# Graph layer on one core: the query rows of 56 of 98 edge tiles come by indexed gather instead of a spreading product, and two bulk blocks are handled earlier

## The chip, the core and the metric

The kernel runs on one core of a Trainium2 chip. The metric is the device time of one execution in microseconds (us), as the median of several runs. Lower is better. TensorE (PE) multiplies matrices, ScalarE (ACT) and VectorE (DVE) work on tiles of 128 partitions, GpSimd (POOL) here mostly issues indexed DMAs, and SyncE (SP) issues plain DMAs.

## What is computed

Two graph layers over 50,000 nodes with 256 features and 12,500 edges sorted by destination. Only nodes that have an incoming edge get more than a constant added:

```python
h = jnp.maximum(_layernorm(x, axis=-1), 0.0)
x = x + _L0_gnn_ref(h, L0_gnn_weight, src, dst, edge_weight)   # relu(segment_sum(w * (h @ W)[src], dst))
h = jnp.maximum(_layernorm(x, axis=-1), 0.0)
x = x + _L1_gnn_ref(h, ...)
# in _L1_gnn_ref:
Q = (h @ Wq).reshape(n, H, HD); K = (h @ Wk)...; V = (h @ Wv)...        # H = 8 heads of 32
score = jnp.einsum('ehd,ehd->eh', Q[dst], K[src]) / np.sqrt(HD)
score = score + jax.nn.relu(efeat @ W1 + b1) @ W2 + b2
alpha = softmax of score over the edges of one dst
out = jax.ops.segment_sum(alpha[:, :, None] * V[src], dst, num_segments=n)
return out.reshape(n, D) @ Wo + bo
```

## The kernel before

The edges are padded to `T = 98` tiles of 128 edges (`P`), in `G = 14` groups of `J = 7` tiles. A run is the set of neighbouring edges with one destination; what belongs to a destination (its x1, its h2, its q row) is complete only in the row of the run's last edge, its *end row*. The program has four stages, each written out in a fixed order for each engine; semaphores tie the engines together.

1. **Edges** (0 to about 363 us in the profile). For each tile: gather of x rows, normalisation, the first layer, second normalisation, q rows. x1, h2 and q are written to DRAM (`x1_d`, `h2_d`, `q_d`). After this stage GpSimd waits until all of h2 is stored.
2. **Pairs** (about 368 to 618 us), the loop `for t in range(T + 1)` on PE and ACT, `pairs` on DVE. For each tile t GpSimd gathers 128 rows of `h2_d` by source into `store` (`fetch`, index `slot_i`). PE transposes them (two products on `ident`), ACT copies the result to `hT`, PE makes K (bank 6 or 7) and V (bank 2 or 3) with `Wkv`, ACT copies V over `store`, DVE multiplies K by the q row of each edge's destination (`prod`, counted by `k3`) and sums over each head.

   Where the q rows come from: SP loads the group's rows of `q_d` linearly into `ringA` (`q_in`). There only end rows are right, so PE *spreads* them: a product of a 0/1 matrix `same` (DVE, `same_run`, from the positions of the end rows, `run_ends`) with the tile in `ringA` puts into each edge's row the end row of its run (bank 0 or 1), and ACT copies it to `msg`. A run that goes on in the next tile has its end row elsewhere; for that case GpSimd gathers one row per tile (`q_open`, index `end_i`), SP writes these rows over row 127 of each tile in `q_d`, and for the first 14 tiles a second time into `ringA` (`open_to`), for which PE waits before its first spread.
3. **Softmax** over runs (about 618 to 669 us), while the last bulk blocks are moved.
4. **Attend** (about 670 us to the end): weighted V, running sums, product with `Wo`, and GpSimd scatters the rows of each tile to `out`.

**Bulk.** Independent of the edges, out = x + bo is made for all nodes in 44 blocks ("units") of 9 rows per partition (1152 KB each): `bulk_load`, `add_bo`, `bulk_store`, in buffers of a rotation (`bulk_at`). Units 0 to 13 have their add on GpSimd in the edges stage, units 14 (`EARLY`) to 37 on DVE in the pairs stage (`add_unit` at j = 2 and j = 5 of a group, as many as `units(g)` has), 38 (`MIDDLE`) to 43 are filled with bo by ACT (`fill`) and added to by an accumulating load of GpSimd's queue. On SP, a bulk store waits for its add, and the load two units later is written behind it.

The rings: `ringA` holds 14 tiles (`A(u)`); gathers into `store` stay at most 14 tiles ahead of PE's transposes (`need(pool, t3, t - 2 * J + 1)`).

Of the kernel before, what the change touches and what calls it, by code (L numbers as in the profile page):

```python
# [8 lines left out]
P = 128  # L9
# [27 lines left out]
def gnn_program(nc, x, dst, src, wgt, eattr, W, Wq, Wk, Wv, W1, b1, W2, b2, Wo, bo, out):  # L37
# [9 lines left out]
    h2_d = nc.dram_tensor("h2", (EP, D), f32, kind="Internal").ap()  # L47
    q_d = nc.dram_tensor("q", (EP, D), f32, kind="Internal").ap()
    srcf_d = nc.dram_tensor("src_f", (T, P), u16, kind="Internal").ap()
    end_d = nc.dram_tensor("run_end", (EP,), bf16, kind="Internal").ap()  # L50
# [3 lines left out]
    with ctx:  # L54
        def sb(name, shape, dt=f32):
            return ctx.enter_context(nc.sbuf_tensor(name, shape, dt))
# [4 lines left out]
        def sem(name):  # L61
            return ctx.enter_context(nc.semaphore(name))
# [34 lines left out]
        slot_i = sb("slot_gather", [P, T], i32)  # L97
        end_i = sb("run_end_after", [T, 1], i32)
        row_no = sb("row_no", [P, 1])
        sc_all = sb("scores", [P, J, G, H])  # L100
# [66 lines left out]
        def group(ring, b):  # L167
            return ring[:, b * J * D:(b + 1) * J * D].rearrange("p (j d) -> p j d", d=D)
# [4 lines left out]
        def keys_ps(j):  # L173
# [28 lines left out]
        ql, end_in = sem2("q_loaded"), sem2("run_ends_in")  # L202
        s_end, end_out, open_in, open_out, open_to = (sem(n) for n in (
            "run_ends_ready", "run_ends_in_dram", "open_q_in", "open_q_in_dram", "open_q_in_ring"))
        same_rdy, qs, qc = (sem(n) for n in ("same_run_ready", "q_spread_in_psum", "q_spread_ready"))
        lag3, s_bo, s_reach = sem("dve_lag3"), sem("bo_parts_step"), sem("reach_of_carries")
        rb_free = sem("masks_in_ringB_used")
        s_flag, x_ps, x_sb, s_sm, pe_sm, act_sm, al_ps, s_al = (sem(n) for n in (
# [64 lines left out]
        def units(g):  # L273

            k = MIDDLE - EARLY
            return range(EARLY + k * g // G, EARLY + k * (g + 1) // G)

# [38 lines left out]
        def _(sp):  # L316
# [80 lines left out]
            def q_in(a):  # L397
                sp.dma_start(group(ringA, a % 2), edge_rows(q_d, a)).then_inc(ql[a % 2], 16)

            sp.wait_ge(keys, T)  # L400
            for a in range(2):
                ends_in(a)
            bulk_load(EARLY)
            bulk_load(EARLY + 1)
            sp.wait_ge(h1, T)
            for i in range(2):
                sp.wait_ge(st_q[i], 32)
            for a in range(2):
                q_in(a)
            for a in range(2):  # L410
                sp.wait_ge(ql[a], 16)
            sp.wait_ge(open_in, 16)
            sp.dma_start(q_d.rearrange("(t p) d -> t p d", p=P)[:, P - 1, :], q_open).then_inc(open_out, 16)
            sp.wait_ge(open_out, 16)
            sp.dma_start(ringA[P - 1:P, :].rearrange("o (u d) -> o u d", d=D),
                         q_d.rearrange("(t p) d -> p t d", p=P)[P - 1:P, 0:2 * J, :]).then_inc(open_to, 16)
            bulk_load(EARLY + 2)
            sp.wait_ge(x1r, T)
# [8 lines left out]
            for g in range(G):  # L427
                for u in units(g):
                    bulk_store(u)
                    if EARLY < u < MIDDLE - 2:  # L430
                        bulk_load(u + 2)
                if g + 2 < G:
                    sp.wait_ge(same_rdy, g + 1)
                    ends_in(g + 2)
                    sp.wait_ge(qs, J * (g + 1))
                    q_in(g + 2)
# [15 lines left out]
        def _(pool):  # L452
# [47 lines left out]
            for i in range(2):  # L500
                for part in range(2):
                    pool.wait_ge(st_h[part][i], 16 * (G // 2))
            for t in range(T):
                if t == 4:
                    for i in range(2):
                        pool.wait_ge(st_q[i], 16 * G)
                    fetch(q_open, q_d, end_i[:, 0:1], open_in)
                need(pool, t3, t - 2 * J + 1)
                u = t % (2 * J)
                fetch(store[:, t * D:(t + 1) * D], h2_d, slot_i[:, t:t + 1], o_in[u],  # L510
                      bounds_check=EP - 1, oob_is_err=False)

# [16 lines left out]
        def _(act):  # L529
# [111 lines left out]
            for t in range(T + 1):  # L641
                if t < T:
                    act.wait_ge(t3, t + 1)
                    need(act, kv, t - 1)
                    nc.scalar.copy(hT[t % 2], bank[4 + t % 2][:, 0:D].rearrange("p (c e) -> p c e", c=NC)).then_inc(hT3, 1)
                if t > 0:
                    act.wait_ge(qs, t)
                    need(act, k3, t - 2)
                    nc.scalar.copy(msg(t - 1), bank[(t - 1) % 2][:, 0:D]).then_inc(qc, 1)
                    act.wait_ge(kv, t)  # L650
                    nc.scalar.copy(store[:, (t - 1) * D:t * D], bank[2 + (t - 1) % 2][:, 0:D]).then_inc(v3, 1)  # L651
# [33 lines left out]
        def _(dve):  # L685
# [62 lines left out]
            def edges(g, h, b, on):  # L748
# [21 lines left out]
                def slots(j):  # L770
# [14 lines left out]
                    ins.then_inc(keys_rd, 1)  # L785

                for j in range(J):
                    u, t = b * J + j, J * g + j
# [58 lines left out]
            def same_run(a):  # L847

                dve.wait_ge(end_in[a % 2], 16 * (a // 2 + 1))
                need(dve, qs, J * (a - 1))  # L850
                nc.vector.tensor_scalar(same[a % 2], run_ends[a % 2], row_no[:, :], None, ALU.is_equal).then_inc(same_rdy, 1)
# [15 lines left out]
            def pairs(g, h, b, on):  # L867
# [16 lines left out]
                if g == 0:  # L884
                    same_run(0)
                for j in range(J + 1):
                    if j < J:
                        t = J * g + j
                        dve.wait_ge(kv, t + 1)
                        dve.wait_ge(qc, t + 1)  # L890
                        nc.vector.tensor_tensor(prod[:, j, :], bank[6 + t % 2][:, 0:D], msg(t), ALU.mult).then_inc(k3, 1)  # L891
                    if j == 3 and g + 1 < G:
                        same_run(g + 1)
# [122 lines left out]
        def _(pe):  # L1016
# [10 lines left out]
            pe.wait_ge(s_nxt, 2)  # L1027
            mm(bank[7][0:T, 0:1], line[:, 2, 1:T + 1], one_row[0:1, 0:1]).then_inc(s_tr, 1)
            pe.wait_ge(pdve, 12)
            pe.wait_ge(s_mlp, 144)  # L1030
# [91 lines left out]
            for t in range(T + 1):  # L1122
# [112 lines left out]
```

## Time and profile before

| | |
|---|---|
| median of 3 runs | 818.31 us (816.94 to 819.22) |
| the profiled execution | 815.25 us, span 813.1 us |
| busy share PE, DVE, ACT, POOL | 85%, 71%, 58%, 62% |
| mean granted TensorE clock | 0.963 |

The span is the time from the first to the last instruction in the trace; 815.25 - 813.1 = 2.15 us lie around it. Busy shares are averages over four stages with different limits.

### The profile page before, as it was taken

To read this page: it belongs to the slowest core of one execution; us is meant where nothing else is said; L and a number is where in the kernel's file an instruction comes from. 1 tells how busy PE (TensorE), PEld (TensorE's weight loads), DVE (VectorE), ACT (ScalarE), POOL (GpSimd) and SP (SyncE) were. 2 spreads that over 40 slices of the span, in tenths; PEclk is the share of its full clock that TensorE was granted. 3 is DMA by queue.
4 is the path that set the end of the run, shared out by engine and by line. 5 is a ranking of instruction groups with operands and counts; after the bars stand their busy time and mean duration, and the time that the engine had idled before them with its cause. 6 is when DMAs were issued, how large, how long until landed. Compare 5 with 4: busy or idle time off the path is not lost.

```text
span 813.1 us, 13370 instructions
## 1 busy us (share of the span) xinstructions
PE 694.8 (85%) x3804; PEld 546.8 (67%) x3804; DVE 580.4 (71%) x1676; ACT 467.7 (58%) x1383; POOL 506.1 (62%) x429
## 2 busy tenths in 40 slices
PE   1578999999799899962999999999998759999990
PEld 0346666666566667742878888888887637777770
DVE  5598888888877676700587565566567859999990
ACT  1557888887588789750444444444446276777700
POOL 6788887788878865206767576566402005777773
PEclk9989999999999999995999999999999978999996
DMA  6688999999989999696479799799796995766751
GB/s 176 212 272 261 335 326 338 354 356 334 321 246 340 312 341 357 231 358 202 151 258 329 275 362 355 283 328 374 253 351 187 269 316 168 222 202 215 231 170 52
DMA packets 122581, 224.01 MB, mean 276 GB/s; under 512 B 27475, under 2 KB 100828, under 8 KB 112142
## 3 DMA queue, kind: packets, MB, share of 16 engines
q1 hardware_dynamic: 74238, 150.45, 54.1%
q0 software_dynamic: 20464, 45.19, 18.6%
q10 hardware_dynamic: 27808, 27.53, 9.7%
q8 instruction: 32, 0.52, 0.2%
q14 instruction: 39, 0.32, 0.1%
HBM read 133.06 MB, written 102.76 MB: 290 GB/s over the span
## 4 chain that ended last, share of the span: by engine, by line
PE 49%; DVE 19%; DMA 15%; ACT 6%; issue 5%; POOL 3%; ACTq 1%; SPq 0%; DVEq 0%; POOLq 0%
PE bank L1018 43%; DVE small L1002 9%; DMA q<-ringC 5%; PE bank L1128 3%; DMA ringB<-x 2%; ACT ringB L623 2%; DVE small L801 2%; DVE store L991 2%; DMA work<-in_x 2%; PE bank L1109 2%; POOL out_x L522 2%; DMA ringA<-in_x,first_src 2%; DVE ringA L982 2%; PE bank L1084 1%; DMA out_x<-work 1%
## 5 line engine op out<-in xcount | busy, mean ns | idle before, releaser
L472 POOL DMA_INDIRECT store<-h,slot_gather x98 | 141.0, 1439 | 107.5 <-PE bank L1128 53.4
L1018 PE MATMUL bank<-Wkv_sb,small 128*128 128x256 f32 x784 | 186.6, 381 | 1.7 <-issue 1.7
L1018 PEld LDWEIGHTS bank<-Wkv_sb,small 128*128 128x128 f32 x784 | 149.9, 191 | 22.8 <-issue 2.1
L522 POOL DMA_INDIRECT out_x<-store,out_scatter x98 | 97.2, 991 | 52.5 <-issue 42.7
L472 POOL DMA_INDIRECT ringC<-in_x,dst_gather x98 | 92.7, 946 | 40.9 <-issue 25.6
L891 DVE TENSOR_TENSOR work<-bank,msgs 128x256 f32<-128x256 f32 x98 | 41.3, 422 | 107.6 <-PE bank L1018 107.6
L651 ACT COPY store<-bank 128x256 f32<-128x256 f32 x98 | 36.5, 372 | 134.3 <-PE bank L1018 134.3
L1018 PE MATMUL bank<-Wo_sb,small 128*128 128x256 f32 x392 | 109.7, 404 | 4.4 <-DVE small L1002 4.4
L679 ACT ACTIVATE ringA<-store,scores 128x32 f32<-128x32 f32 x392 | 87.6, 307 | 33.4 <-PE bank L1196 29.5
L1018 PE MATMUL bank<-W_sb,small 128*128 128x256 f32 x392 | 104.0, 389 | 0.0
L1018 PE MATMUL bank<-Wq_sb,small 128*128 128x256 f32 x392 | 101.5, 382 | 1.7 <-ACT ringC L555 1.6
L472 POOL DMA_INDIRECT ringA<-in_x,src_gather x84 | 79.6, 948 | 24.9 <-issue 19.7
L1002 DVE TENSOR_TENSOR_SCAN small<-flags,small,bank 128x128 f32<-128x128 bf16 x196 | 83.0, 466 | 4.2 <-PE bank L1196 3.6
L801 DVE TENSOR_TENSOR_SCAN small<-flags,small,bank 128x128 f32<-128x128 bf16 x196 | 82.8, 464 | 0.6 <-issue 0.3
L1018 PEld LDWEIGHTS bank<-Wo_sb,small 128*128 128x128 f32 x392 | 69.1, 197 | 16.3 <-DVE small L1002 7.4
L1018 PEld LDWEIGHTS bank<-Wq_sb,small 128*128 128x128 f32 x392 | 67.4, 192 | 7.6 <-issue 2.4
L1018 PEld LDWEIGHTS bank<-W_sb,small 128*128 128x128 f32 x392 | 68.8, 196 | 5.5
L776 DVE SCALAR_TENSOR_TENSOR bank<-bank,src_col,iota 128x128 f32<-128x128 f32 x98 | 34.3, 350 | 53.5 <-PE bank L1018 48.4
L305 POOL TENSOR_TENSOR bulk<-bulk,bo_all 128x2304 f32<-128x2304 f32 x14 | 71.2, 5085 | 0.3
L610 ACT ACTIVATE store<-ringA,nm,rs 128x256 f32<-128x256 f32 x98 | 57.2, 602 | 19.8 <-DVE nm L810 19.8
L1109 PE MATMUL bank<-ident,msgs 128*128 128x128 f32 x196 | 39.7, 285 | 20.7 <-DVE small L801 11.2
L623 ACT ACTIVATE ringB<-ringB,nm,rs 128x256 f32<-128x256 f32 x98 | 54.0, 593 | 1.2 <-DVE nm L836 0.6
(184 smaller groups left out, 1271.0 us busy)
## 6 DMA issues: line engine op xcount, KB each, us to landing
out_x<-bulk SPq DMA_DIRECT2D x33, 1152.0 KB, 7.6
bulk<-in_x SPq DMA_DIRECT2D x30, 1152.0 KB, 9.7
ringA<-q SPq DMA_DIRECT2D x14, 896.0 KB, 10.3
ringB<-x SPq DMA_DIRECT2D x12, 896.0 KB, 5.6
out_x<-ringC SPq DMA_DIRECT2D x9, 1152.0 KB, 6.5
ringC<-in_x SPq DMA_DIRECT2D x8, 1152.0 KB
x<-ringB SPq DMA_DIRECT2D x14, 512.0 KB, 5.9
h<-ringB ACTq DMA_DIRECT2D x14, 512.0 KB, 5.3
```

Of the source, the lines that this page charges most:

```text
L305: ins = eng_ops.tensor_tensor(v, v, bob[0:piece.shape[0], None, :].to_broadcast([piece.shape[0], rows_n, D]), ALU.add)
L472: pool.indirect_dma_start(to, None, table, bass.IndirectOffsetOnAxis(ap=at, axis=0), **more).then_inc(landed, 16)
L522: pool.indirect_dma_start(out, bass.IndirectOffsetOnAxis(ap=out_i[:, t:t + 1], axis=0), store[:, t * D:(t + 1) * D], None, bounds_check=N ...
L610: nc.scalar.activation(store3[:, J * a + k:J * a + k + 1, :], A(ab * J + k)[:, None, :], ACT.Relu, bias=nm1[:, ab, k:k + 1], scale=rs1[:, ...
L623: nc.scalar.activation(B(u), B(u), ACT.Relu, bias=nm2[:, lb, k:k + 1], scale=rs2[:, lb, k:k + 1]).then_inc(h2r, 1)
L651: nc.scalar.copy(store[:, (t - 1) * D:t * D], bank[2 + (t - 1) % 2][:, 0:D]).then_inc(v3, 1)
L679: ins = nc.scalar.activation(A(t % (2 * J))[:, n * HD:(n + 1) * HD], store[:, at:at + HD], ACT.Copy, scale=sc_all[:, t % J, t // J, n:n + 1])
L801: ins = nc.vector.tensor_tensor_scan(aT[u % 2][:, c, :], goes_on(u), bank[0][:, c * P:(c + 1) * P], aT[(u + 1) % 2][:, c, P - 1:P], ALU.mu ...
L891: nc.vector.tensor_tensor(prod[:, j, :], bank[6 + t % 2][:, 0:D], msg(t), ALU.mult).then_inc(k3, 1)
L1002: ins = nc.vector.tensor_tensor_scan(aT[u % 2][:, c, :], goes_on(u), bank[u % 2][:, c * P:(c + 1) * P], aT[(u + 1) % 2][:, c, P - 1:P], AL ...
L1018: return nc.tensor.matmul(o, lhsT, rhs, start=start, stop=stop)
L1109: ins = nc.tensor.transpose(bank[0][:, c * P:(c + 1) * P], msg(u + 1)[:, c * P:(c + 1) * P], ident[:, :])
```

## The change

- A tile t is now *spread* only if t >= 14 and t is even (42 tiles, `spread`). For the 56 others (`q_at` picks the column of the index table `qg_i`) GpSimd gathers the q rows of the end rows straight into `ringA`, 4 tiles behind its gathers into `store` (`lead`), and DVE multiplies K by `ringA` directly. PE's spreading product and ACT's copy to `msg` are gone for these tiles.
- `qg_i` is made at the start: PE transposes `w_last` into bank 4, DVE copies 14 and 42 columns of it.
- `q_in` loads only the rows of the spread tiles of groups 2 to 13, 127 rows of each, and the 128th from a table of its own, `open_d`. `same_run` runs for groups 2 to 13. The chain by way of `q_d` and `open_to` is gone.
- Units 14 and 15 are added to by DVE before its first tile, stored by SP before it waits for the last stores of q, and units 16 and 17 loaded behind that. `units(g)` shares out 22 units, not 24.

```diff
         def units(g):
-            k = MIDDLE - EARLY
-            return range(EARLY + k * g // G, EARLY + k * (g + 1) // G)
+            k = MIDDLE - EARLY - 2
+            return range(EARLY + 2 + k * g // G, EARLY + 2 + k * (g + 1) // G)
+        def spread(t):
+            return t >= 2 * J and t % 2 == 0
+        def spreads(t):
+            return max(0, (t - 2 * J + 1) // 2)
+        def q_at(t):
+            return t if t < 2 * J else J + t // 2
+        def q_landed(t):
+            return 16 * (T // (2 * J) + t // (2 * J) + 1)
...
             def q_in(a):
-                sp.dma_start(group(ringA, a % 2), edge_rows(q_d, a)).then_inc(ql[a % 2], 16)
+                rows_in = group(ringA, a % 2)[:, a % 2::2, :]
+                sp.dma_start(rows_in[0:P - 1], edge_rows(q_d, a)[0:P - 1, a % 2::2, :]).then_inc(ql[a % 2], 16)
+                sp.dma_start(rows_in[P - 1:P], open_d[J * a + a % 2:J * (a + 1):2, :][None, :, :]).then_inc(ql[a % 2], 16)
             sp.wait_ge(keys, T)
-            for a in range(2):
+            for a in (2, 3):
                 ends_in(a)
-            bulk_load(EARLY)
-            bulk_load(EARLY + 1)
-            sp.wait_ge(h1, T)
+            for u in range(EARLY, EARLY + 2):
+                bulk_load(u)
+            for u in range(EARLY, EARLY + 2):
+                bulk_store(u)
             for i in range(2):
-                sp.wait_ge(st_q[i], 32)
-            for a in range(2):
-                q_in(a)
-            for a in range(2):
-                sp.wait_ge(ql[a], 16)
+                sp.wait_ge(st_q[i], 16 * G)
+            for u in range(EARLY + 2, EARLY + 4):
+                bulk_load(u)
             sp.wait_ge(open_in, 16)
-            sp.dma_start(q_d.rearrange("(t p) d -> t p d", p=P)[:, P - 1, :], q_open).then_inc(open_out, 16)
-            sp.wait_ge(open_out, 16)
-            sp.dma_start(ringA[P - 1:P, :].rearrange("o (u d) -> o u d", d=D),
-                         q_d.rearrange("(t p) d -> p t d", p=P)[P - 1:P, 0:2 * J, :]).then_inc(open_to, 16)
-            bulk_load(EARLY + 2)
+            sp.dma_start(open_d, q_open).then_inc(open_out, 16)
...
-                    sp.wait_ge(same_rdy, g + 1)
-                    ends_in(g + 2)
-                    sp.wait_ge(qs, J * (g + 1))
+                    if g == 0:
+                        sp.wait_ge(open_out, 16)
+                    if g >= 2:
+                        sp.wait_ge(same_rdy, g - 1)
+                        ends_in(g + 2)
+                        sp.wait_ge(qs, spreads(J * (g + 1)))
+                    else:
+                        sp.wait_ge(k3, J * (g + 1))
                     q_in(g + 2)
...
-            for t in range(T):
-                if t == 4:
+            lead = 4
+            for t in range(T + lead):
+                if t < T:
+                    need(pool, t3, t - 2 * J + 1)
+                    fetch(store[:, t * D:(t + 1) * D], h2_d, slot_i[:, t:t + 1], o_in[t % (2 * J)],
+                          bounds_check=EP - 1, oob_is_err=False)
+                v = t - lead
+                if v == 0:
                     for i in range(2):
                         pool.wait_ge(st_q[i], 16 * G)
+                    pool.wait_ge(h1, T)
+                    pool.wait_ge(s_qg, 1)
+                if v >= 0 and not spread(v):
+                    need(pool, k3, v - 2 * J + 1)
+                    fetch(A(v % (2 * J)), q_d, qg_i[:, q_at(v):q_at(v) + 1], x_in[v % (2 * J)])
+                if v == 5:
                     fetch(q_open, q_d, end_i[:, 0:1], open_in)
...
                 if g == 0:
-                    same_run(0)
+                    for u in range(EARLY, EARLY + 2):
+                        add_unit(u)
...
-                        dve.wait_ge(qc, t + 1)
-                        nc.vector.tensor_tensor(prod[:, j, :], bank[6 + t % 2][:, 0:D], msg(t), ALU.mult).then_inc(k3, 1)
+                        if spread(t):
+                            q_rows = msg(spreads(t))
+                            dve.wait_ge(qc, spreads(t) + 1)
+                        else:
+                            q_rows = A(t % (2 * J))
+                            dve.wait_ge(x_in[t % (2 * J)], q_landed(t))
+                        nc.vector.tensor_tensor(prod[:, j, :], bank[6 + t % 2][:, 0:D], q_rows, ALU.mult).then_inc(k3, 1)
...
-                    if v % J == 0:
-                        pe.wait_ge(same_rdy, v // J + 1)
-                        pe.wait_ge(ql[v // J % 2], 16 * (v // J // 2 + 1))
-                        pe.wait_ge(open_to, 16)
-                    need(pe, qc, v - 1)
-                    mm(bank[v % 2][:, 0:D], same[v // J % 2][:, v % J * P:(v % J + 1) * P], A(v % (2 * J))).then_inc(qs, 1)
+                    if spread(v):
+                        a, n = v // J, spreads(v)
+                        if v < J * a + 2:
+                            pe.wait_ge(same_rdy, a - 1)
+                            pe.wait_ge(ql[a % 2], 32 * (a // 2))
+                        need(pe, qc, n - 1)
+                        mm(bank[n % 2][:, 0:D], same[a % 2][:, v % J * P:(v % J + 1) * P], A(v % (2 * J))).then_inc(qs, 1)
```

What stands on GpSimd's queue from the end of the edges stage to the bulk loads behind the pairs stage (`ringC<-in_x` are the last gathers of the edges stage, `store<-h` is a gather by source, `small<-q,run_end_after` the open rows, x94 is 94 in a row), before:

```order
L472 DMA ringC<-in_x,dst_gather 128x256 x3
L305 TENSOR_TENSOR bulk<-bulk,bo_all 128x2304
L472 DMA store<-h,slot_gather 128x256 x4
L472 DMA small<-q,run_end_after 98x256
L472 DMA store<-h,slot_gather 128x256 x94
L516 DMA bulk<-in_x 128x2x1152
```

and in the changed kernel, from the same place:

```order
L493 DMA ringC<-in_x,dst_gather 128x256 x3
L324 TENSOR_TENSOR bulk<-bulk,bo_all 128x2304
L493 DMA store<-h,slot_gather 128x256 x5
L493 DMA ringA<-q,q_gather 128x256
L493 DMA store<-h,slot_gather 128x256
L493 DMA ringA<-q,q_gather 128x256
L493 DMA store<-h,slot_gather 128x256
```

and its last gathers of the stage, where two into `store` stand between two of q:

```order
L493 DMA ringA<-q,q_gather 128x256
L493 DMA store<-h,slot_gather 128x256 x2
L493 DMA ringA<-q,q_gather 128x256
L493 DMA store<-h,slot_gather 128x256 x2
L493 DMA ringA<-q,q_gather 128x256 x3
L545 DMA bulk<-in_x 128x2x1152
```

Ninety-nine indexed DMAs have become 155, and the open rows moved behind ten gathers into `store` and six of q. VectorE between the edges stage and the third tile of the pairs stage, before (L851 is `same_run`, L891 the product with q, L896 the sum over heads, L305 `add_bo`):

```order
L836 SCALAR_TENSOR_TENSOR nm<-mv,rs 128x7
L851 TENSOR_SCALAR hid<-work,row_no 128x896
L891 TENSOR_TENSOR work<-bank,msgs 128x256 x2
L896 TENSOR_REDUCE ssum<-work 128x8
L891 TENSOR_TENSOR work<-bank,msgs 128x256
L896 TENSOR_REDUCE ssum<-work 128x8
L305 TENSOR_TENSOR bulk<-bulk,bo_all 128x2304
```

and in the changed kernel (`add_bo` is L324, the product L932):

```order
L871 SCALAR_TENSOR_TENSOR nm<-mv,rs 128x7
L324 TENSOR_TENSOR bulk<-bulk,bo_all 128x2304 x2
L932 TENSOR_TENSOR work<-bank,ringA 128x256 x2
L937 TENSOR_REDUCE ssum<-work 128x8
L932 TENSOR_TENSOR work<-bank,ringA 128x256
L937 TENSOR_REDUCE ssum<-work 128x8
L324 TENSOR_TENSOR ringC<-ringC,bo_all 128x2304
```

Two bulk adds stand now ahead of the first product, and `same_run` of group 0 is gone; the next bulk add stands where it stood.

## Rows read from the trace of the kernel before

**Rows 1.** Busy time by stage: us, PE, PEld, DVE, ACT, POOL, clock, DMA share, GB/s

```profile
340.00:370.00 30.00, 18.72 (x108) 13.76 (x100) 5.47 (x24) 15.09 (x43) 1.29 (x2) 0.96 0.93 331
...
364.00:368.00 4.00, 0.00 (x0) 0.00 (x0) 0.00 (x0) 0.00 (x0) 0.00 (x0) 0.97 1.09 385
...
370.00:382.00 12.00, 1.82 (x6) 1.39 (x7) 0.00 (x0) 0.74 (x2) 8.73 (x9) 0.50 0.32 88
460.00:500.00 40.00, 40.00 (x204) 34.83 (x203) 26.42 (x45) 17.08 (x51) 27.61 (x17) 1.00 0.93 332
```

**Rows 2.** Chain of work in order of time, start and length, pairs stage's ends

```profile
357.50 10.04 DMA h<-ringB
...
374.25 2.65 DMA small<-q,run_end_after
...
376.96 1.68 DMA q<-small
378.67 2.46 DMA ringA<-q
...
381.26 4.17 PE bank L1018 x10
385.43 0.22 PE bank L1128 x2
385.65 2.16 PE bank L1018 x10
...
617.96 0.37 ACT store L651
618.33 2.01 ACT bulk L657
```

**Rows 3.** Who waited for whom: us in total, times, longest

```profile
POOL store L472 <- PE bank L1128: 53.4, 41, 2.6
POOL ringA L472 <- issue: 23.4, 82, 0.3
```

**Rows 4.** GpSimd in order of time, start and length, pairs stage

```profile
368.40 1.03 POOL L472 DMA_INDIRECT store<-h,slot_gather  x1 [36.43 <-DMA h<-ringB]
369.74 1.00 POOL L472 DMA_INDIRECT store<-h,slot_gather  x1 [0.30 <-issue]
...
414.97 3.13 POOL L472 DMA_INDIRECT store<-h,slot_gather  x1 [1.22 <-PE bank L1128]
...
437.00 1.00 POOL L472 DMA_INDIRECT store<-h,slot_gather  x1 [0.30 <-issue]
438.32 1.54 POOL L472 DMA_INDIRECT store<-h,slot_gather  x1 [0.32 <-issue]
```

**Rows 5.** VectorE in order of time, beside these gathers and at the stage's end

```profile
414.69 2.55 DVE L305 TENSOR_TENSOR ringC<-ringC,bo_all 128x2304 f32<-128x2304 f32 x1
...
436.98 2.07 DVE L878 TENSOR_TENSOR_SCAN ringB<-ringB 112x896 bf16<-112x896 bf16 x1
...
618.94 0.42 DVE L891 TENSOR_TENSOR work<-bank,msgs 128x256 f32<-128x256 f32 x1
```

**Rows 6.** Costliest groups of the page: xcount, busy us, mean ns

```profile
L472 POOL DMA_INDIRECT ringA<-in_x,src_gather x84 | 79.6, 948 | 24.9 <-issue 19.7
```

**Rows 7.** DMA landing times: bulk and ringA at 344 to 381, store at 382 to 617

```profile
DMA to landing us min/median/max: 10.2/10.3/10.3
DMA to landing us min/median/max: 14.5/16.5/18.5
DMA to landing us min/median/max: 2.4/7.3/12.1
```

**Rows 8.** SyncE's DMA issues in order of time

```profile
348.18 3.57 SPq L350 DMA_DIRECT2D bulk<-in_x  x2
351.88 3.67 SPq L398 DMA_DIRECT2D ringA<-q  x2
```

More of the change, by code:

```diff
@@ L48, in gnn_program @@
     q_d = nc.dram_tensor("q", (EP, D), f32, kind="Internal").ap()
+    open_d = nc.dram_tensor("q_open_rows", (T, D), f32, kind="Internal").ap()
     srcf_d = nc.dram_tensor("src_f", (T, P), u16, kind="Internal").ap()
@@ L98, in gnn_program @@
         end_i = sb("run_end_after", [T, 1], i32)
+        qg_i = sb("q_gather", [P, J + T // 2], i32)
         row_no = sb("row_no", [P, 1])
@@ L202, in gnn_program @@
         ql, end_in = sem2("q_loaded"), sem2("run_ends_in")
-        s_end, end_out, open_in, open_out, open_to = (sem(n) for n in (
-            "run_ends_ready", "run_ends_in_dram", "open_q_in", "open_q_in_dram", "open_q_in_ring"))
+        s_end, end_out, open_in, open_out = (sem(n) for n in (
+            "run_ends_ready", "run_ends_in_dram", "open_q_in", "open_q_in_dram"))
         same_rdy, qs, qc = (sem(n) for n in ("same_run_ready", "q_spread_in_psum", "q_spread_ready"))
         lag3, s_bo, s_reach = sem("dve_lag3"), sem("bo_parts_step"), sem("reach_of_carries")
+        s_qg = sem("q_gather_ready")
         rb_free = sem("masks_in_ringB_used")
@@ L429, in _ @@
                     bulk_store(u)
-                    if EARLY < u < MIDDLE - 2:
+                    if u < MIDDLE - 2:
                         bulk_load(u + 2)
                 if g + 2 < G:
-                    sp.wait_ge(same_rdy, g + 1)
-                    ends_in(g + 2)
-                    sp.wait_ge(qs, J * (g + 1))
+                    if g == 0:
[6 more added lines that the diff above has]
+                        sp.wait_ge(k3, J * (g + 1))
                     q_in(g + 2)
@@ L502, in _ @@
                     pool.wait_ge(st_h[part][i], 16 * (G // 2))
-            for t in range(T):
-                if t == 4:
+            lead = 4
[6 more added lines that the diff above has]
+                if v == 0:
                     for i in range(2):
                         pool.wait_ge(st_q[i], 16 * G)
+                    pool.wait_ge(h1, T)
[4 more added lines that the diff above has]
+                if v == 5:
                     fetch(q_open, q_d, end_i[:, 0:1], open_in)
[L508 to L511, printed above, removed]
             for u in range(MIDDLE, BULK + 1):
@@ L646, in _ @@
                 if t > 0:
-                    act.wait_ge(qs, t)
-                    need(act, k3, t - 2)
-                    nc.scalar.copy(msg(t - 1), bank[(t - 1) % 2][:, 0:D]).then_inc(qc, 1)
+                    if spread(t - 1):
+                        n = spreads(t - 1)
+                        act.wait_ge(qs, n + 1)
+                        need(act, k3, t - 4 if n > 1 else 0)
+                        nc.scalar.copy(msg(n), bank[n % 2][:, 0:D]).then_inc(qc, 1)
                     act.wait_ge(kv, t)
@@ L785, in slots @@
                     ins.then_inc(keys_rd, 1)
+                if g == -1:
+                    dve.wait_ge(s_tr, 8)
+                    nc.vector.tensor_copy(qg_i[:, 0:2 * J], bank[4][:, 2 * P:2 * P + 2 * J])
+                    nc.vector.tensor_copy(qg_i[:, 2 * J:], bank[4][:, 2 * P + 2 * J + 1:2 * P + T:2]).then_inc(s_qg, 1)
                 for j in range(J):
@@ L847, in same_run @@
             def same_run(a):
-                dve.wait_ge(end_in[a % 2], 16 * (a // 2 + 1))
-                need(dve, qs, J * (a - 1))
+                dve.wait_ge(end_in[a % 2], 16 * (a // 2))
+                need(dve, qs, spreads(J * (a - 1)))
                 nc.vector.tensor_scalar(same[a % 2], run_ends[a % 2], row_no[:, :], None, ALU.is_equal).then_inc(same_rdy, 1)
@@ L889, in pairs @@
                         dve.wait_ge(kv, t + 1)
-                        dve.wait_ge(qc, t + 1)
-                        nc.vector.tensor_tensor(prod[:, j, :], bank[6 + t % 2][:, 0:D], msg(t), ALU.mult).then_inc(k3, 1)
-                    if j == 3 and g + 1 < G:
+                        if spread(t):
[5 more added lines that the diff above has]
+                        nc.vector.tensor_tensor(prod[:, j, :], bank[6 + t % 2][:, 0:D], q_rows, ALU.mult).then_inc(k3, 1)
+                    if j == 3 and 2 <= g + 1 < G:
                         same_run(g + 1)
@@ L1028, in _ @@
             mm(bank[7][0:T, 0:1], line[:, 2, 1:T + 1], one_row[0:1, 0:1]).then_inc(s_tr, 1)
+            pe.wait_ge(s_end, 1)
+            nc.tensor.transpose(bank[4][:, 2 * P:2 * P + T], w_last, ident[0:T, 0:T]).then_inc(s_tr, 1)
             pe.wait_ge(pdve, 12)
```

## Prediction

> **What bounds the kernel now.** I read the busy time by stage first, for the reader to see that the pairs stage is TensorE's: from 460 to 500 us PE is busy in all 40 us at a granted clock of 1.00, DVE in 26.4, ACT in 17.1, GpSimd in 27.6, and the DMA share is 0.93, near full but not full [rows 1]. The chain of waits says the same in order of time: from 381.26 to 617.96 it runs on PE alone, in a beat of 0.22 us (two transposes) and 2.16 us (ten instructions, so 0.216 each: every f32 product of 128x256 is two of them, four products make K and V, one spreads q) [rows 2]. That is 2.38 us a tile, 16.66 us a group of seven. The list of waits shows GpSimd with room beside it: 53.4 us idle in 41 waits for PE [rows 3]. Ahead of the stage stands a second limit. The last h2 store lands at 367.5, the first gather starts at 368.40; then comes the detour of the open rows (gather 2.65, store 1.68, load 2.46 us), and only at 381.26 does PE take its first spread [rows 2, 4]. Behind the stage ACT's last copy of V at 617.96 is followed by ACT's fill at 618.33, which starts the last bulk transfers [rows 2]. The softmax and attend stages hang on that time and are not edited, so the end of the pairs stage moves the end of the kernel one for one.
>
> **PE and ACT.** 56 tiles lose the spreading product, 2 x 0.216 = 0.43 us each: 24 us. PE's floor for the stage is 56 x 1.95 + 42 x 2.38 = 209 us instead of 98 x 2.38 = 233. ACT loses 56 copies of 0.37 us, which lay beside PE's work and give nothing. If PE stayed the bound and also began earlier, the gain would be near 30 us. So the question is what GpSimd does with 56 more gathers.
>
> **GpSimd.** A gather into `store` takes 1.00 us and the next starts 0.30 later, a pitch of 1.30 [rows 4]. A gather into `ringA` without a bounds check took 948 ns in the edges stage, with the same 0.3 us to the next: 1.25 [rows 3, 6]. I take that for the q gathers. A group from the third on has 7 x 1.30 + 3.5 x 1.25 = 13.5 us of gathers; the first two have 7 x 2.55 = 17.9, already more than the 16.66 of before. To this come the bulk adds of VectorE. The add at 414.69 lasts 2.55 us; the gather that starts at 414.97 lasts 3.13 instead of 1.00 and ends 0.86 us after the add [rows 4, 5]. So a gather that starts d after an add's start loses 2.55 + 0.86 - 1.00 - d = 2.41 - d. The scan at 436.98 tells who is hit: the gather at 437.00 ran its 1.00 us beside it unhindered, the one at 438.32 took 1.54 [rows 4, 5]. A gather needs what the add holds only at its beginning. Before, GpSimd often waited for the same PE event as DVE, so d was mostly 0.28, and the time lost came out of idle time. Now GpSimd has no idle time, and the next gather begins anywhere in 0 to 1.3 us after an add's start: 1.77 us lost on average, bounds 1.1 and 2.41.
>
> The Trainium skill ("SBUF — State Buffer", Who interferes with whom) says that a VectorE instruction with two SBUF inputs contends with a GpSimd instruction that reads SBUF, and that the first to start holds the ports for its whole length. The held gather agrees with it, with 3.13 us against 1.00; the scan that ran beside the gather at 437.00 does not.
>
> 22 adds are left in the stage. The last two stand at tiles 93 and 96, where GpSimd has issued its last gathers (it issues q three tiles ahead of its use), so 20 hit: 35.4 us. Two long scans of DVE (2.07) cost 1.25 each by the same rule, twelve `same_run` 0.1 each: 3.7 us.
>
> **The start.** SP no longer issues the two ring loads (896 KB each, at 351.9 to 355.5, landing after 14.5 and 18.5 us) into the stretch in which the DMA share is 1.09 at 385 GB/s and GpSimd waits for h2 [rows 1, 7, 8]. 1.8 MB are 4.7 us of traffic. Against that, the bulk loads issued from 348.2 land after 10.3 us, near 358.5 and 361.6 [rows 7, 8]; DVE adds 2.55 us to each while it has nothing else to do, and their stores (1.15 MB each) go out at about 361 and 364, partly ahead of the landing of h2. I take the first gather 3 us earlier, at 365.4; bounds 4.7 earlier and 1 later. The adds themselves are over by 364.2 and hold up no gather. PE no longer waits for the open rows. The index table costs two DVE copies and a transpose near the program's start, 0.5 us under waits for loads; I count nothing, with 0.5 as the cost if that cover is missing. The open rows now come some 20 us later on SP; what is queued behind them (the flags, the store of unit 16, the first half load of q) is wanted by tile 14 or later, about 420 us, and SP is through by 396.
>
> **The sum.** The first gather at 365.4; 98 x 1.30 = 127.4; 55 q gathers before the last one, 68.8; open rows 1.3; 0.6 for the waits ahead of q; stalls 35.4 + 3.7. The last q gather starts at 602.6. It lands 7.3 us later (the median in this stage, between 2.4 and 12.1) [rows 7]: 609.9. The gather before it, for tile 95, lands at 608.6; DVE's product frees the bank (0.42), PE makes K and V of tile 97 (1.73), ACT copies V (0.37): ACT is free at 611.2, against 618.33. DVE's own branch (product of 96, a sum, the bulk add, product of 97) has its last product at 612.3 against 618.94 [rows 5]. So the stage ends 7 us earlier, the profiled execution would take 815.25 - 7 = 808.3, and against the median of 818.31, which lies 3.1 above that execution, 811.3.
>
> Put differently: gained are some 8 us at the start and 5 us at the end, where the four leading gathers into `store` are done; lost are 3 to 4 us in each of the first two groups; each later group takes 13.5 + 1.5 x 1.77 + 0.3 = 16.4 us, hardly less than 16.66. Nearly all of PE's 24 us turn into waits of PE for GpSimd.
>
> Half and whole clock: in the idle stretch before the stage the granted clock was 0.50, in the stages with PEld near two thirds it was 0.96 to 1.00 [rows 1]. PE will now idle a few tenths of a us a tile; I expect 1.00 and no cost.
>
> **Rivals.**
> - *Full stalls (slower).* Adds follow the landing of a gather, and landings follow GpSimd's beat, so the two may lock together with d near 0. Then each add costs 2.41: 20 x 0.64 = 12.8 us more, 824.1. It is slower by more than 0.3% once an add costs over 2.25 on average. For it speaks that almost every held gather of before lost over 2 us; against it, that these had one releaser. 0.20.
> - *The gather holds, too (no change).* If a gather kept its hold for its whole 1.00 us, an add would start at its end, and the next gather 0.3 us behind the add: 2.12 lost each, 7 us more in all, 818.3. An earlier start that does not come (h2 held up by the two bulk stores) gives 814 to 816 alone and the same with a part of this. 0.18. The skill's rule of the first to start, taken at its word, is this case.
> - *Short stalls (much faster).* If adds mostly come just after a gather has begun, or where GpSimd has none to issue, each costs 1.1 or less: 13 us less, 798; the floor is PE's, near 788. 0.14.
> - *The forecast:* 811.3, own range 806 to 815.5. 0.48.
>
> A measurement of this kernel tells apart about 0.3%, 2.5 us. Faster by more: 0.48 + 0.14 = 0.62; within: 0.18; slower: 0.20. The range of 8 in 10 goes from 800, in the short stalls, to 820, in the full ones.
>
> **What the profile after would show.** GpSimd busy with hardly an idle wait for PE from 366 to 603, gathers into `ringA` near 0.95 us, 20 of either kind over 2 us; PE's waits now for DVE's product, which waits for a DMA into `ringA`; tiles 2.5 to 3 us apart up to tile 13; chain of waits through GpSimd instead of PE; DMA share over 0.85. Wrong would be: a gather of q slower than 1.1 us beside `store` gathers (each 0.1 is 5.6 us), landings of 10 us, a late bulk load that stops DVE, a first gather after 368, or GpSimd waiting for ring places.

## The result, and the profile after

The changed kernel took 972.67 us as the median of 4 runs (968.56 to 983.36), the kernel before 817.62. The ratio is 1.190 (95% interval 1.181 to 1.199): 19% slower, where I had forecast 0.9% faster. The profiled execution took 968.56 us, its span is 966.6.

The page of the profile after, its first two parts (busy time, then the span in 40 slices of 24.2 us):

```profile
PE 704.6 (73%) x3693; PEld 547.9 (57%) x3693; DVE 581.4 (60%) x1676; ACT 447.1 (46%) x1327; POOL 553.6 (57%) x485
...
PE   1779999999998967735585455581846886899991
...
POOL 6788888888886407775543354261640011577774
PEclk9989999999999997867777788685987998899996
DMA  7589999999999795564264644363433699667761
```

The stretch of the first load of q that is discussed below, by stage (PE, PEld, DVE, ACT, POOL, clock, DMA share, GB/s):

```profile
391.00:420.00 29.00, 14.07 (x54) 11.07 (x53) 16.54 (x27) 3.98 (x12) 23.16 (x20) 0.79 0.46 158
```

In the pairs stage, slices 15 to 31, nobody is busy. PE stands at 1 to 8 tenths, mostly near 5, GpSimd falls from 7 to between 0 and 6, and the DMA share is about half where it had been 0.93 [rows 1]. Neither GpSimd nor DMA bandwidth as a whole was the bound. The stage runs from the first gather at 359.66 to ACT's first fill at 770.58: 410.9 us against 249.9 [rows 2, 4]. The 161 us are the whole loss. The total shows less of it, as the stage starts 8.7 us earlier: 4.7 because the edges stage happened to end earlier in this execution (last h2 store issued at 352.81, not 357.50), 4.0 by the change.

What PE and GpSimd wait for, in the list of waits (us in total, times, longest):

```profile
PE bank L1059 <- issue: 140.0, 14, 20.5
POOL store L493 <- PE bank L1171: 111.9, 31, 22.2
...
DVE work L932 <- DMA ringA<-q,q_gather: 28.4, 6, 17.1
...
PE bank L1059 <- DMA ringA<-q_open_rows: 16.5, 1, 16.5
```

"Issue" names no releaser that the profile can tie. In order of time these waits stand ahead of the first spread of each group: 11 of 2 to 20.5 us for groups 3 to 13 and the 16.5 us for group 2, twelve in a stage with 12 group loads, 148 us together. SyncE's own queue shows it, in order of time:

```profile
389.98 0.43 SPq L369 DMA_DIRECT2D bulk<-in_x  x1
390.51 0.46 SPq L418 DMA_DIRECT2D ringA<-q  x1
391.02 29.08 SPq L419 DMA_DIRECT2D ringA<-q_open_rows  x1
420.15 0.44 SPq L378 DMA_DIRECT2D out_x<-bulk  x1
...
429.87 0.38 SPq L418 DMA_DIRECT2D ringA<-q  x1
430.29 20.91 SPq L419 DMA_DIRECT2D ringA<-q_open_rows  x1
```

L418 is the load of 127 rows of q, L419 the one-partition load of 3 or 4 open rows (3 or 4 KB). The tiny one sits in SyncE for 26 to 29 us in a group with four spread tiles and 19 to 21 us in one with three, twelve times. All bulk stores and loads stand behind it. The chain of waits in order of time shows PE standing until both loads of the group are there (they count on one semaphore, and the profile names the later issue):

```profile
391.02 35.48 DMA ringA<-q_open_rows
426.50 0.14 issue
426.64 4.60 PE bank L1059 x10
...
446.66 11.45 issue
...
473.44 14.50 issue
```

The q rows of group 2, issued at 390.5, are there at 426.5. The load for group g + 2 is issued behind the last spread of group g, so it has one group's time, 16.7 us, to land. 36 us don't fit. There is a smaller loss on top: after the wait PE's ten instructions take 4.60 us, where they take 2.16 in the beat, at a granted clock of 0.50, the lower of the two levels (1.2 GHz). The twelve restarts together cost about 26 us, an estimate from the chain's rows.

### The profile page after: what moved, and what is told of

The parts are those of the page before. It is cut to its first block, busy times and chain, and to the rows that moved or that the text cites. A ratio compares the mean times of both kernels' runs of the same rounds, so it can differ in the third digit from the quotient of the medians.

```text
span 966.6 us, 13083 instructions
## 1 busy us (share of the span) xinstructions
PE 704.6 (73%) x3693; PEld 547.9 (57%) x3693; DVE 581.4 (60%) x1676; ACT 447.1 (46%) x1327; POOL 553.6 (57%) x485
## 3 DMA queue, kind: packets, MB, share of 16 engines
q1 hardware_dynamic: 66584, 142.64, 42.7%
## 4 chain that ended last, share of the span: by engine, by line
PE 40%; issue 19%; DVE 17%; DMA 12%; ACT 6%; POOL 4%; ACTq 1%; SPq 1%; DVEq 0%; POOLq 0%
PE bank L1059 34%; DVE small L1043 7%; DMA ringA<-q_open_rows 4%; DVE small L836 2%; DMA ringB<-x 2%; ACT ringB L652 2%; PE bank L1171 2%; DMA q<-ringC 2%; POOL ringA L493 2%; PE bank L1152 2%; DMA work<-in_x 2%; DVE store L1032 2%; PE bank L1127 1%; DVE ringA L1023 1%; POOL out_x L551 1%
## 5 line engine op out<-in xcount | busy, mean ns | idle before, releaser
L493 POOL DMA_INDIRECT store<-h,slot_gather x98 | 129.3, 1319 | 180.8 <-PE bank L1171 111.9
L1059 PE MATMUL bank<-Wkv_sb,small 128*128 128x256 f32 x784 | 211.0, 418 | 9.7 <-issue 8.1
L1059 PEld LDWEIGHTS bank<-Wkv_sb,small 128*128 128x128 f32 x784 | 163.6, 215 | 35.6 <-issue 8.7
L932 DVE TENSOR_TENSOR work<-bank,msgs 128x256 f32<-128x256 f32 x42 | 17.7, 421 | 200.5 <-PE bank L1059 200.5
L1059 PE MATMUL bank<-ringA,hid 128*128 128x256 f32 x48 | 17.9, 460 | 105.4 <-issue 88.9
L680 ACT COPY msgs<-bank 128x256 f32<-128x256 f32 x42 | 15.6, 372 | 157.3 <-PE bank L1059 157.1
L324 POOL TENSOR_TENSOR bulk<-bulk,bo_all 128x2304 f32<-128x2304 f32 x14 | 71.2, 5088 | 0.2
L493 POOL DMA_INDIRECT ringA<-q,q_gather x56 | 59.4, 1060 | 18.5 <-issue 17.9
## 6 DMA issues: line engine op xcount, KB each, us to landing
out_x<-bulk SPq DMA_DIRECT2D x33, 1152.0 KB, 10.2
```

Source lines behind the costliest of these rows:

```text
L324: ins = eng_ops.tensor_tensor(v, v, bob[0:piece.shape[0], None, :].to_broadcast([piece.shape[0], rows_n, D]), ALU.add)
L493: pool.indirect_dma_start(to, None, table, bass.IndirectOffsetOnAxis(ap=at, axis=0), **more).then_inc(landed, 16)
L1059: return nc.tensor.matmul(o, lhsT, rhs, start=start, stop=stop)
```

## The experiments

**Five kernels on the loads of 127 rows.** In `split112` each load is issued as 112 and 15 rows:

```diff
-                sp.dma_start(rows_in[0:P - 1], edge_rows(q_d, a)[0:P - 1, a % 2::2, :]).then_inc(ql[a % 2], 16)
+                for lo, hi in ((0, 112), (112, P - 1)):
+                    sp.dma_start(rows_in[lo:hi], edge_rows(q_d, a)[lo:hi, a % 2::2, :]).then_inc(ql[a % 2], 16)
...
-                            pe.wait_ge(ql[a % 2], 32 * (a // 2))
+                            pe.wait_ge(ql[a % 2], 48 * (a // 2))
```

> The changed kernel, but each load of q for the spread tiles is issued as rows 0 to 111 and rows 112 to 126 in place of one DMA of 127 rows; the one-row DMA of the open rows stays. Theory B (the one-row DMA of 3 or 4 KB is itself what SyncE spends 20 to 29 us on): nothing changes, about 970 us. Theory C (the stage is slow for more gathers on GpSimd, the DMA only follows): about 970 us, with SyncE's issue short.

Measured: 819.55 us (4 runs), ratio to the kernel before 1.006 (0.998 to 1.013). One line about how 127 rows are cut is worth 153 us. SyncE's queue in it:

```profile
403.38 2.96 SPq L419 DMA_DIRECT2D ringA<-q  x2
406.38 0.78 SPq L420 DMA_DIRECT2D ringA<-q_open_rows  x1
...
426.93 1.02 SPq L419 DMA_DIRECT2D ringA<-q  x2
428.00 0.68 SPq L420 DMA_DIRECT2D ringA<-q_open_rows  x1
```

The one-partition load takes 0.6 to 0.8 us now that a load of another shape stands ahead of it, and GpSimd issues as many gathers as before. Theories B and C fall, A stands.

`split122` has 122 in place of 112 in the same lines.

> As before, but rows 0 to 121 and rows 122 to 126. 122 is 2 times 61. 
Measured: 876.89 us (one run). It lies between, as a count of two engines has it, though higher than I had said: SyncE is held longer than 8 to 12 us.

```profile
405.08 16.17 SPq L419 DMA_DIRECT2D ringA<-q  x1
421.29 0.62 SPq L420 DMA_DIRECT2D ringA<-q_open_rows  x1
```

Here it is already the second piece of the load itself (5 rows) that is held behind the first. So it is whatever stands next in SyncE's queue. The first pieces with four spread tiles hold it for 14 to 17 us, those with three for 12 to 14.

`no_open` is the changed kernel without L419 and with waits for 16 in place of 32.

> The changed kernel without the one-row DMA of the open rows into the ring; it leaves out these rows, so edges whose run goes on in the next tile get a stale row. The 127-row DMA stays. Theory A: SyncE's next issue (a bulk store or load) takes the 20 us in its place, PE waits for the rows as before, total 940 to 975 us. Theory B: the wait is gone, total about 810 us.

Measured: 974.09 us (one run). Its SyncE queue, and from its chain of waits the first load of q, for which PE waits alone now:

```profile
435.77 0.35 SPq L418 DMA_DIRECT2D ringA<-q  x1
444.97 12.26 SPq L378 DMA_DIRECT2D out_x<-ringC  x1
```

```profile
397.21 35.38 DMA ringA<-q
```

The bulk store, which starts later because it waits for its add, is held in place of the open rows, until 21.5 us after the issue of the load. The load of 127 rows lands 35.4 us after its issue with no open rows behind it. So the open rows cost nothing that shows (974 us against 973).

`before127` puts only that shape into the kernel before:

```diff
-                sp.dma_start(group(ringA, a % 2), edge_rows(q_d, a)).then_inc(ql[a % 2], 16)
+                for lo, hi in ((0, P - 1), (P - 1, P)):
+                    sp.dma_start(group(ringA, a % 2)[lo:hi], edge_rows(q_d, a)[lo:hi]).then_inc(ql[a % 2], 16)
...
-                        pe.wait_ge(ql[v // J % 2], 16 * (v // J // 2 + 1))
+                        pe.wait_ge(ql[v // J % 2], 32 * (v // J // 2 + 1))
```

> The kernel before, but its 14 ring loads of seven tiles are each issued as rows 0 to 126 and row 127. Nothing of the rest of the change is in it. Theory A: 889 KB at 23 GB/s are 39 us for each group in place of the 16.7 us that a group takes, 22 us lost in each of 14 groups, total about 1100 to 1150 us. Theory C: no difference from the kernel before, 815 to 820 us.

Measured: 1262.12 us (one run), 447 us more than the kernel before, so 32 us a group where I had worked out 22. The shape alone does it, without any gather of q.

```profile
507.28 41.52 SPq L399 DMA_DIRECT2D ringA<-q  x2
```

In the wait behind it there are 15 us in which no engine does anything and only this load moves (busy time by stage, the last two numbers are the share of the 16 DMA engines and GB/s):

```profile
530.00:545.00 15.00, 0.00 (x0) 0.00 (x0) 0.00 (x0) 0.00 (x0) 0.00 (x0) 0.50 0.07 24
```

A share of 0.07 is one engine of 16 (0.0625). The load ran on one DMA engine, at 24 GB/s. In `split122` a us with little else in it has twice that, two engines:

```profile
419.00:420.00 1.00, 0.75 (x4) 0.70 (x5) 1.00 (x4) 0.00 (x0) 0.87 (x1) 1.00 0.13 47
```

At 24 GB/s alone, 508 KB would take 22 us (an estimate from that row). They took 36, and from 391 to 401 us and again from 420 to 430 the bulk transfers beside them brought the DMA share to 0.89 to 0.96. That this one engine served both by turns would fit, but no run separates it.

`split126` issues 126 rows and one.

> Loads of q as rows 0 to 125 and row 126. 126 is 9 times 14. If the number of engines is the largest divisor up to 16, it is 14, and it runs as with 112 rows, 812 to 826 us. If only multiples of 16 rows spread over more engines, it runs as with 127 rows, 970 us.

Measured: 821.02 us (one run). Multiples of 16 are not needed; 126 rows are as good as 112: SyncE takes 1 to 3 us for both pieces and 0.6 for the open rows.

Four counts then: 112 and 126 rows no hold, 122 rows up to 17 us, 127 rows up to 29 us. The Trainium skill ("DMA: Bandwidth & Descriptors", Why a DMA increments its semaphore by 16 and not by 1) says that a DMA is spread over the largest number of engines, at most 16, that divides the outermost size: 16 for 112, 14 for 126, 2 for 122, 1 for 127. The times agree with this order, and the shares of 0.07 and 0.13 with the 1 and the 2. The 16 and the 14 were not read from a trace.

**The rest of the change, once the loads are mended.** `split112` is not faster than the kernel before, against my forecast for just this. Five kernels ask where that gain is. `psum_bo` takes away what I had as GpSimd's main loss, the second SBUF input of the bulk adds; bo stands in a PSUM bank that the spreading product gives up (shown against `split112`):

```diff
-                ins = eng_ops.tensor_tensor(v, v, bob[0:piece.shape[0], None, :].to_broadcast([piece.shape[0], rows_n, D]), ALU.add)
+                src_bo = bob[0:piece.shape[0], None, :] if eng is None else bank[1][0:piece.shape[0], None, 0:D]
+                ins = eng_ops.tensor_tensor(v, v, src_bo.to_broadcast([piece.shape[0], rows_n, D]), ALU.add)
...
                 if g == 0:
+                    nc.vector.tensor_copy(bank[1][:, 0:D], bob[:, :]).then_inc(s_bop, 1)
+                    dve.wait_ge(s_bop, 1)
...
-                        need(pe, qc, n - 1)
-                        mm(bank[n % 2][:, 0:D], same[a % 2][:, v % J * P:(v % J + 1) * P], A(v % (2 * J))).then_inc(qs, 1)
+                        need(pe, qc, n)
+                        mm(bank[0][:, 0:D], same[a % 2][:, v % J * P:(v % J + 1) * P], A(v % (2 * J))).then_inc(qs, 1)
```

> The mended kernel (loads of q as 112 + 15 rows) with bo copied once into PSUM bank 1, so that VectorE's bulk adds have one SBUF input in place of two; the spreading product uses bank 0 alone. Theory P (a gather on GpSimd is held when it begins while a VectorE instruction with two SBUF inputs runs; that cost GpSimd about 43 us of gathers' time in the mended kernel, and GpSimd's pace is the stage's): no gather beside an add takes over 1.1 us, the stage gets shorter by 15 to 25 us, total 792 to 806 us. Theory Q (the stage is held by the landing of gathers and by PE): gathers are short, the total stays within 5 us of 819. Theory R (the adds hold GpSimd whatever their inputs): gathers stay at 3 us, no change.

Measured: 804.49 us (6 runs), ratio 0.984 (0.980 to 0.988), 1.6% faster than the kernel before. The groups of instructions in the pairs stage (xcount, busy us, mean ns, idle before), first of `split112`, then of `psum_bo`:

```profile
L494 POOL DMA_INDIRECT store<-h,slot_gather x98 | 123.8, 1263 | 63.1 <-DMA h<-ringB 33.6 <-issue 26.8 <-PE bank L1172 2.7
L494 POOL DMA_INDIRECT ringA<-q,q_gather x56 | 69.9, 1249 | 18.4 <-issue 16.3 <-PE bank L1172 1.5 <-DVE work L933 0.6
```

```profile
L496 POOL DMA_INDIRECT store<-h,slot_gather x98 | 100.5, 1025 | 70.3 <-DMA h<-ringB 33.5 <-issue 26.8 <-PE bank L1176 10.1
L496 POOL DMA_INDIRECT ringA<-q,q_gather x56 | 54.6, 975 | 19.0 <-issue 16.1 <-DVE work L937 1.7 <-PE bank L1176 1.2
```

The gathers lost 23.3 + 15.3 = 38.6 us beside the adds and lose almost nothing now; the adds themselves last 2.55 us in both. Theory P is right, Q and R fall. The total gains 15 us of the 38.6, since PE becomes the bound again: from 440 to 500 us it is busy throughout at a clock of 1.00. It had been busy for 58.6 of these 60 us in `split112` already, so there was not much more to gain: by the prediction's own terms a later group costs GpSimd 16.4 us and PE 3.5 x (1.95 + 2.38) = 15.2, and twelve times the difference is 15 us (an estimate).

```profile
400.00:420.00 20.00, 15.24 (x67) 12.58 (x68) 11.57 (x21) 4.25 (x13) 15.17 (x16) 0.91 0.98 327
420.00:440.00 20.00, 17.30 (x80) 14.47 (x79) 14.15 (x22) 6.12 (x18) 15.99 (x14) 0.91 0.94 321
440.00:500.00 60.00, 60.00 (x307) 52.18 (x306) 41.14 (x74) 23.16 (x70) 45.98 (x47) 1.00 0.90 319
```

(Busy time by stage of `psum_bo`: PE, PEld, DVE, ACT, POOL, clock, DMA share, GB/s.) What is left lies mostly in its first 14 tiles (to about 420 us), where PE has gaps.

`lead2` is `split112` with `lead = 2`.

> The mended kernel with GpSimd's gathers of q 2 tiles behind those into store in place of 4. The first 14 tiles are held by GpSimd's order: every tile of them waits for its q gather, which is issued two places (2.6 us) earlier now. The first product comes 2.6 us earlier. If the first 14 tiles' delay decides: 2 to 3 us faster than the mended kernel, about 816 to 817 us. If GpSimd's total decides: no difference.

Measured: 820.08 us (10 runs), ratio 1.006 (1.002 to 1.010), the same as `split112`. But the run did not do what I had meant it to. GpSimd's queue in it:

```profile
366.37 1.03 POOL L494 DMA_INDIRECT store<-h,slot_gather  x1 [33.52 <-DMA h<-ringB]
...
374.21 0.97 POOL L494 DMA_INDIRECT ringA<-q,q_gather  x1 [4.21 <-issue]
```

The first gather of q starts 7.84 us behind the first one into `store`, in `split112` 7.86: it waits 4.2 us for the last store of q instead. VectorE's first product comes no earlier either (15.8 us behind the first gather, 16.0 in `split112`). So what an earlier product would be worth was not tested.

`early_bulk` is the kernel before with the bulk part of the change alone: `units(g)` over 22 units, DVE's `add_unit` of 14 and 15 behind `same_run(0)`, and on SyncE

```diff
             for a in range(2):
                 q_in(a)
+            for u in range(EARLY, EARLY + 2):
+                bulk_store(u)
             for a in range(2):
                 sp.wait_ge(ql[a], 16)
...
-            bulk_load(EARLY + 2)
+            for u in range(EARLY + 2, EARLY + 4):
+                bulk_load(u)
```

> The kernel before with only the second part of the change: VectorE adds units 14 and 15 before its first tile, SyncE stores them and then loads 16 and 17; 22 units in the groups. PE bounds the pairs stage and the adds lay under its work, so I expect no difference, 813 to 819 us. If the stores of the two units hold up the open rows or the last store of h2 it is 2 to 5 us slower; if the adds matter, up to 5 us faster.

Measured: 822.51 us (10 runs), ratio 1.009 (1.005 to 1.012): slower, where I had expected no difference. GpSimd's queue in it, in order of time:

```profile
368.13 1.00 POOL L475 DMA_INDIRECT store<-h,slot_gather  x1 [0.30 <-issue]
375.24 0.98 POOL L475 DMA_INDIRECT small<-q,run_end_after  x1 [6.11 <-issue]
```

The fetch of the open rows waits 6.1 us for the last store of q, 0.9 us in the kernel before. The chain of waits of `early_bulk` shows that store at 358.41 with 14.30 us. From the issue of that store to the fetch it is 16.8 us, in the kernel before 10.5 (363.74 to 374.25).

`early_late_store` moves the two stores behind the loads that PE waits for (against `early_bulk`):

```diff
-            for u in range(EARLY, EARLY + 2):
-                bulk_store(u)
...
+            for u in range(EARLY, EARLY + 2):
+                bulk_store(u)
             for u in range(EARLY + 2, EARLY + 4):
                 bulk_load(u)
```

> The kernel before with units 14 and 15 added to early, as in early_bulk (which was 0.85% slower), but their stores issued behind the load of the open rows into the ring, so behind the last store of q. Theory S (the two stores of 1.15 MB held up the last store of q, on which the open rows and PE's first spread wait: 16.8 us from its issue to the fetch of the open rows in place of 10.5): the 6.5 us come back, 812 to 819 us, ratio to the kernel before within 0.4% of 1. Theory T (22 adds in the groups in place of 24, or the later loads, cost the time): stays 5 to 8 us slower.

Measured: 811.27 us (12 runs), ratio 0.997 (0.993 to 1.002). The loss is gone, and from that store of q to the fetch it is 10.2 us again; whether a small gain is left can't be told. Theory S holds. `psum_late_store` is `psum_bo` with the two stores behind the wait for the last stores of q.

> The version with bo in PSUM, with the stores of units 14 and 15 issued behind the wait for the last store of q. GpSimd's wait ahead of its first q gather (1.7 us) and a part of the time to the last h2 store fall away: 1 to 4 us faster than with the stores ahead, 800 to 804 us. If the early stores hold up nothing here, no difference; if the later loads of 16 to 18 come too late for VectorE's adds, up to 5 us slower.

Measured: 808.10 us (6 runs), ratio 0.987 (0.983 to 0.992), not distinct from `psum_bo`. GpSimd's wait ahead of its first gather of q is gone (0.3 us, 1.7 in `psum_bo`), but the 1 to 4 us that I had expected of it do not show.

## Why the prediction was wrong, point by point

**The step that failed** is in the part on the start, where I let SyncE be "through by 396" with "the first half load of q", and in the sum, where the 12 new loads of q have no term, so cost nothing. I had counted their bytes, half of before, and their number, and had not looked at their shape. The old load moved 128 partitions, the new one 127. What stood in place of nothing: each load runs on one DMA engine of 16 and takes 36 us to land where one group's time is 16.7, and the stage is 161 us longer. The runs put the whole loss there: `split112` takes away 153 of 155 us, and `before127` makes such a loss from nothing else. The loss has two ways of action at once. The load lands 36 us after its issue, so PE stands before the first spreading product of each group; and whatever SyncE issues next is held for 20 to 29 us, so bulk loads and stores, DVE's adds behind them, and the places in `ringA` come late as well. PE's twelve waits for landings are 148 us; how much of them comes from loads that are issued late behind the hold was not separated, as `no_open` shows both still at work. No rival of mine held it, and so neither did the range. The Trainium skill ("DMA: Bandwidth & Descriptors", the section named above) states the rule on divisors; the trace of before does not show it, as it has no load of such a shape on that path.

**GpSimd as the new pace.** Right in kind for the mended kernel, with PE close behind it. From the first gather to the start of the last q gather I had 365.4 to 602.6, 237.2 us; `split112` has 371.86 to 613.89, 242.0. Pitches of 1.30 and 1.25 us came out as read (948 ns forecast for the gather of q, 0.95 to 0.96 measured unhindered).

**The stalls.** `psum_bo` takes away the stalls of the adds alone, so its 38.6 us stand against the 35.4 of the sum. 20 adds hit a gather in `split112`, as forecast, for 1.93 us each on average, not 1.77. What `psum_bo` keeps, beside scans and `same_run`, is 3.5 us, where I had 3.7. With 1.93 the full stalls (2.41) and the short stalls (1.1) are both excluded. The mean alone, half way between 1.77 and 2.12, does not exclude that a gather holds an add, but the rows of `split112` do:

```profile
420.30 1.01 POOL L494 DMA_INDIRECT store<-h,slot_gather  x1 [0.31 <-issue]
420.79 2.55 DVE L324 TENSOR_TENSOR bulk<-bulk,bo_all 128x2304 f32<-128x2304 f32 x1
421.61 2.62 POOL L494 DMA_INDIRECT store<-h,slot_gather  x1 [0.30 <-issue]
```

The add begins 0.49 us into a gather and neither is longer than alone; the next gather is held. Nine of the 20 adds began so, all of 2.55 us. So a gather is held only when it begins, and the rival of the gather that holds, too, does not happen here.

**The start.** From the issue of the last h2 store to the first gather 10.9 us before (357.50 to 368.40), 7.9 in `split112` (363.96 to 371.86): the 3 us that I took. But I saw only h2. The stores of units 14 and 15 slow the last store of q; in the kernel before this costs 6 us (`early_bulk`), in the mended one GpSimd waits 1.6 us ahead of its first q gather, where I had 0.9 with the usual gap.

**The end.** ACT's fill begins 12.6 us after the start of the last q gather in `split112`, not 8.6 (611.2 less 602.6). I had one bulk add of DVE on this path; both stand on it, as PE's K and V of the last tiles wait for DVE's products between them:

```profile
618.82 0.42 DVE L933 TENSOR_TENSOR work<-bank,ringA 128x256 f32<-128x256 f32 x1 [5.11 <-DMA ringA<-q,q_gather]
619.16 0.41 DVE L938 TENSOR_REDUCE ssum<-work 128x8 f32<-128x256 f32 x1
619.49 2.55 DVE L324 TENSOR_TENSOR bulk<-bulk,bo_all 128x2304 f32<-128x2304 f32 x1
621.95 0.42 DVE L933 TENSOR_TENSOR work<-bank,msgs 128x256 f32<-128x256 f32 x1
...
625.14 2.55 DVE L324 TENSOR_TENSOR ringC<-ringC,bo_all 128x2304 f32<-128x2304 f32 x1
627.61 0.42 DVE L933 TENSOR_TENSOR work<-bank,ringA 128x256 f32<-128x256 f32 x1
```

5 us for GpSimd and 4 for the end turn my 4 us shorter stage (245.8 against 249.9) into one of 254.6 in this execution. So even without the shape of the loads the change would not have brought the 7 us.

**The clock.** I had expected 1.00 and no cost. In `split112` the granted clock is 0.82 from 372 to 400 us and 0.91 from 400 to 440. After waits of 2.3 to 3.3 us PE's eight instructions of 1.73 us take 3.5 to 3.7, three times:

```profile
429.67 3.25 issue
432.91 3.65 PE bank L1060 x8
```

That is some 5.5 us of PE's time, which in part lies under its waits for GpSimd.

**Open** is how much of `psum_bo`'s remaining stage could go. VectorE waits for landings of q gathers 23 times in `split112`, 71.9 us, one of them the 17.2 us before its first product. The 17 waits behind 420 us (42.7 us) are gone in `psum_bo`; the six in the first 14 tiles stay (29.5 us, 16.8 of them before the first product). There every tile needs two gathers, 2.55 us of GpSimd, and 1.95 of PE, so some of this is GpSimd's pace. No run brought the first product forward or changed that pace.

## What to carry to other kernels

Look at the outermost size of each DMA that a change touches, not only at its bytes: 127 partitions instead of 128 made a load of half the bytes 36 us long, and cutting the same 127 rows as 112 + 15 or 126 + 1 took that away. When a tiny DMA seems to take tens of us in its issuing queue, suspect the one ahead of it. And when gathers move to GpSimd in a stage in which VectorE adds SBUF to SBUF, count each such add as a stall of the gathers, or move one of its inputs to PSUM; here that turned a change worth nothing into 1.6%. What it would give the kernel before, where GpSimd had idle time, was not tested.

## What the runs showed of the hardware that I had not expected

- A load of 508 KB in 127 partitions landed 36 us after its issue, about 14 GB/s, while the whole core moved 158 GB/s in the first 29 us of it. With nothing beside it such a load moved 24 GB/s at a DMA share of 0.07, one engine of 16 (`before127`). The DMA issued next on the same queue left SyncE only 20 to 30 us after it, whatever it was: a load of 4 KB, or a bulk store.
- The same queue held for 12 to 17 us behind 122 partitions, and for at most 3 us behind 126 or 112.
- A bulk add of VectorE with one input in PSUM lasts the same 2.55 us as with both in SBUF but lets indexed gathers go on: their mean falls from 1263 to 1025 ns. The Trainium skill ("SBUF — State Buffer", Who interferes with whom) has two SBUF inputs as what contends with GpSimd's reads, which agrees; it also says that a `tensor_tensor` was not seen to stall a DMA of GpSimd, with which the gathers of 2.3 to 3.6 us beside the adds of `split112` do not agree. A gather already under way neither held an add nor was held by it (nine cases).
